# A two-layer conditioned token mixer on one core: fourteen groups of unread matmuls left out, and the last tiles' steps placed anew

## The chip, the cores and the metric

The kernel runs on one core of one Trainium2 chip. The metric is the device time of one execution in microseconds (us). Before the change three timed runs gave 438.00, 437.63 and 439.25 us, so the median is 438.0 us.

## The reference, cut to what matters

Two layers act on x (2 batches of 1024 tokens, 256 features), with one condition vector and 154 context rows per batch.

```python
# layer 0: attention over the context, router, gate and three experts
nx = layer_norm(x) * gamma + beta
weights = softmax((nx @ Wq) @ (context @ Wk).T / 16)
evidence = weights @ (context @ Wv)
combined = concat([nx, evidence, condition])            # 768 features
probs = softmax(combined @ router_W + router_b)         # 3 experts
h = silu(combined @ e_w1[e] + e_b1[e])                  # 512 per expert
routed = sum_e probs[e] * (h @ e_w2[e] + e_b2[e])
g = sigmoid(silu(combined @ gate_w1 + gate_b1) @ gate_w2 + gate_b2)
x = x + g * (routed @ out_w + out_b)
# layer 1: adaptive layer norm, attention with 16 heads of 16 features
q = ada_ln(x, condition) @ Wq + bq
k, v = split(ada_ln(context, condition) @ Wkv + bkv)
x = x + concat_heads(softmax(q k.T / 4) v) @ Wp + bp
```

The output is x, in f32.

## The kernel before

The 2048 tokens are cut into 8 tiles of 256 (t from 0 to 7, four to a batch). Weights, keys and values are prepared once and stay in the on-chip memory. Many products are made exact by splitting both operands into a high and a low part and taking three products, high by high, low by high and high by low (the helper `exact`, lines 1688, 1689 and 1690).

For each tile the work runs through these steps, named in the code by a short key. A key such as ("score", 6, 3) means step score of tile 6, part 3.

- Layer 0: ln, norm, low, att, prob, route and logit make the normalized tokens, their attention over the context and the router. za and z fill one of two hidden banks on TensorE in two halves, in seven units u. ScalarE (also called z) takes the tanh, VectorE (z) finishes the silu, ScalarE (h) makes the high part, GpSimd (h) the low part, and TensorE multiplies both (p) into the token bank. evac adds the token bank to the expert sum. init puts the router-weighted expert biases into that sum, on VectorE, lines 1395 and 1397. res closes the layer.
- Layer 1: qn, shift, xhat, qx, qlow and query normalize the tokens anew and make the queries. stack copies them with DMAs into the stacked form. most computes scores of head pairs and VectorE takes the maximum of each. row turns these maxima around. score computes the scores again with the maxima subtracted, twelve parts of a 128x512 bank, and ScalarE takes their exponential into a ring of six. value multiplies by the values, four parts. raw copies out, sum adds up the softmax denominators (GpSimd), sums is their reciprocal, dup and out spread and multiply them (VectorE), out on ScalarE makes the high part, outl on VectorE the low part, and proj is the last product. For the last tile proj is cut into lead (its first two groups of heads) and last (the other two, in two halves of tokens). Each ends with an addition to the tokens on VectorE and a DMA to the output.

Layer 0 of tile t runs beside layer 1 of tile t-1. After the last part of ("p", 7, 6) nothing of layer 0 is left, and TensorE has only layer 1 of tiles 6 and 7.

**What sets the order.** Nothing is scheduled at run time. Each step has a slot, a number: FIRST + 14 t plus the number in PLAN, or in PLAN_OF for a single tile. For each engine the slot plus the number in DELAY is sorted, and the steps are written in that order into the engine's own instruction stream. Only the relative size of the numbers matters. Each step waits on semaphores for what it reads and for the buffers that it overwrites. Three banks of scores are shared by most, row and score in that order of use, so a score waits until the step three places before it has been read.

**fill.** The step fill, on TensorE alone, is a group of four products of 128x128 by 128x256 into the token bank (line 2129). Nobody reads them, and no semaphore is signalled. There are 14 groups with slots 120.23 to 131.47, all behind ("evac", 7, 3), the last reader of the token bank. Groups 0 to 6 stand among the scores of tile 6, groups 7 and 8 among those of tile 7, and groups 9 to 13 ahead of ("proj", 6).

## Time and profile before

| | |
|---|---|
| median of three runs | 438.0 us (437.63 to 439.25) |
| the profiled execution's own time | 439.08 us |
| its span, first to last instruction | 436.9 us |
| TensorE matmul busy | 422.1 us, 97% |
| TensorE weight load busy | 384.7 us, 88% |
| VectorE busy | 296.3 us, 68% |
| ScalarE busy | 223.6 us, 51% |
| GpSimd busy | 175.0 us, 40% |
| mean granted TensorE clock | 0.996 of full |

In the profile PE is TensorE's matmul, PEld its weight load, DVE is VectorE, ACT is ScalarE, POOL is GpSimd and SP is the engine that issues DMAs. The clock is a share of full speed: 1.00 is 2.4 GHz and 0.50 is 1.2 GHz. Busy time says what an engine did, not what set the end. A matmul's row spans its whole latency, so rows that follow each other overlap, and the pace is the distance of their starts.

### The profile page before, as it was taken

The numbers are of one execution on the slowest core, as the hardware profiler recorded it, in microseconds if no ns is written. First come the engines' busy times: TensorE is split into PE (matmuls) and PEld (weight loads), VectorE is DVE, ScalarE is ACT, GpSimd is POOL, SyncE is SP. The second block draws the span as 40 slices with busy tenths as digits, with TensorE's granted clock in tenths as the row PEclk, the third lists the DMA queues.
The fourth block names the chain that finished last, engine by engine and source line by source line (L and its number), as shares of the span: only waits on it lengthen the run. The fifth ranks groups of instructions, "written<-read, shape, count | busy, mean of one in ns | idle before, by whom it ended". The sixth has DMA issues, their size and how long they took to land.

```text
span 436.9 us, 9623 instructions
## 1 busy us (share of the span) xinstructions
PE 422.1 (97%) x3629; PEld 384.7 (88%) x3629; DVE 296.3 (68%) x748; ACT 223.6 (51%) x487; POOL 175.0 (40%) x184
## 2 busy tenths in 40 slices
PE   7899999999999999999999999999999899979996
PEld 6578999989998899889998899889988898868876
DVE  2785566674675696739863797389658755891797
ACT  2868643255347543764367246724672356326271
POOL 4545474553353526324523344344433632330020
PEclk9999999999999999999999999999999999998999
DMA  8786102531100210023000300030003021300301
GB/s 288 252 298 269 50 2 47 142 91 31 44 5 1 63 59 30 24 78 116 2 5 13 109 1 5 14 86 0 5 20 80 0 56 28 80 3 26 72 3 48
DMA packets 16837, 27.80 MB, mean 64 GB/s; under 512 B 3800, under 2 KB 9112, under 8 KB 16664
## 3 DMA queue, kind: packets, MB, share of 16 engines
q1 hardware_dynamic: 16664, 27.19, 21.2%
q8 instruction: 29, 0.48, 0.5%
q14 instruction: 16, 0.13, 0.1%
q10 hardware_dynamic: 128, 0.01, 0.0%
HBM read 15.94 MB, written 2.10 MB: 41 GB/s over the span
## 4 chain that ended last, share of the span: by engine, by line
PE 77%; DVE 15%; issue 3%; ACT 3%; DMA 1%; SPq 1%; ACTq 0%
PE hidden_banks L1688 7%; PE hidden_banks L1690 7%; PE hidden_banks L1689 7%; PE score_banks L1695 6%; PE score_banks L2060 5%; PE token_bank L1688 5%; PE token_bank L1689 5%; PE token_bank L1690 5%; PE score_banks L2030 4%; PE value_bank L2083 3%; PE value_bank L2086 3%; PE value_bank L1695 3%; DVE head_maxima L1463 3%; PE hidden_banks L1913 2%; DVE sums L1477 2%
## 5 line engine op out<-in xcount | busy, mean ns | idle before, releaser
L1620 POOL TENSOR_TENSOR hidden_low<-hidden,hidden_high 128x512 fp32r<-128x512 f32 x56 | 72.8, 1300 | 123.5 <-ACT hidden_high L1072 123.4
L1463 DVE TENSOR_REDUCE head_maxima<-score_banks 128x2 f32<-128x308 f32 x128 | 54.6, 473 | 17.1 <-PE score_banks L2030 15.0
L1688 PE MATMUL hidden_banks<-normed_high,hidden_w_high 128*128 128x256 f32 x224 | 64.2, 287 | 0.8 <-issue 0.8
L1689 PE MATMUL hidden_banks<-normed_high,hidden_w_low 128*128 128x256 f32 x224 | 62.5, 279 | 0.0
L1690 PE MATMUL hidden_banks<-normed_low,hidden_w_high 128*128 128x256 f32 x224 | 62.5, 279 | 0.0
L1132 ACT ACTIVATE exp_ring<-score_banks 128x512 f32<-128x512 f32 x96 | 52.6, 600 | 18.8 <-PE score_banks L2060 17.5
L1072 ACT CAST hidden_high<-hidden 128x512 fp32r<-128x512 f32 x56 | 34.8, 622 | 48.2 <-DVE hidden L1380 48.1
L1688 PE MATMUL token_bank<-expert_out_high,hidden_high 128*128 128x256 f32 x192 | 55.7, 290 | 0.0
L1064 ACT ACTIVATE hidden<-hidden_banks 128x512 f32<-128x512 f32 x56 | 33.3, 595 | 41.6 <-PE hidden_banks L1913 40.0
L1690 PE MATMUL token_bank<-expert_out_low,hidden_high 128*128 128x256 f32 x192 | 53.4, 278 | 0.0
L1689 PE MATMUL token_bank<-expert_out_high,hidden_low 128*128 128x256 f32 x192 | 53.4, 278 | 0.0
L1380 DVE SCALAR_TENSOR_TENSOR hidden<-hidden,hidden_banks 128x512 f32<-128x512 f32 x56 | 38.2, 683 | 18.5 <-ACT hidden L1064 18.3
L1688 PEld LDWEIGHTS hidden_banks<-normed_high,hidden_w_high 128*128 128x128 f32 x224 | 42.1, 188 | 2.1 <-issue 2.0
L1689 PEld LDWEIGHTS hidden_banks<-normed_high,hidden_w_low 128*128 128x128 f32 x224 | 42.3, 189 | 0.1
L1690 PEld LDWEIGHTS hidden_banks<-normed_low,hidden_w_high 128*128 128x128 f32 x224 | 42.0, 188 | 0.0
L1688 PEld LDWEIGHTS token_bank<-expert_out_high,hidden_high 128*128 128x128 f32 x192 | 36.2, 188 | 0.5 <-issue 0.2
L1689 PEld LDWEIGHTS token_bank<-expert_out_high,hidden_low 128*128 128x128 f32 x192 | 36.3, 189 | 0.2
L1690 PEld LDWEIGHTS token_bank<-expert_out_low,hidden_high 128*128 128x128 f32 x192 | 36.1, 188 | 0.0
L2030 PE MATMUL score_banks<-pair_keys,query_stack 96*128 96x308 f32 x112 | 29.4, 335 | 2.5 <-DVE head_maxima L1463 1.4
L1913 PE MATMUL hidden_banks<-probs_T_tail,context_w_tail 100*128 100x256 f32 x112 | 31.6, 282 | 0.0
L1689 PE MATMUL hidden_banks<-probs_T_high,context_w_low 128*128 128x256 f32 x112 | 31.2, 279 | 0.0
L1688 PE MATMUL hidden_banks<-probs_T_high,context_w_high 128*128 128x256 f32 x112 | 31.2, 279 | 0.0
(294 smaller groups left out, 1111.5 us busy)
## 6 DMA issues: line engine op xcount, KB each, us to landing
unit_weights<-units SPq DMA_DIRECT2D x7, 768.0 KB, 6.0
query_stack<-queries_high SPq DMA_DIRECT2D x56, 64.0 KB, 2.0
tokens<-x SPq DMA_DIRECT2D x8, 256.0 KB, 3.7
query_stack<-queries_low SPq DMA_DIRECT2D x28, 64.0 KB, 2.0
w_slice<-units SPq DMA_DIRECT2D x7, 256.0 KB, 3.0
out<-tokens SPq DMA_DIRECT2D x7, 256.0 KB, 2.4
w_T<-folds SPq DMA_DIRECT2D x6, 256.0 KB, 6.1
pair_keys<-keys_high SPq DMA_DIRECT2D x16, 77.0 KB
```

What stands on the lines that cost most here:

```text
L1064: nc.scalar.activation(TB[:, ring(t, u), :], Z[:, hidden_bank(t, u), :], ACT.Tanh, scale=0.5).then_inc(scalar_z, 1)
L1072: nc.scalar.copy(SH[:, ring(t, u), :], TB[:, ring(t, u), :]).then_inc(scalar_h, 1)
L1132: nc.scalar.activation(E[:, w % ERING, :], S[:, ring_of[key][0], :], ACT.Exp).then_inc(scalar_score, 1)
L1380: v.scalar_tensor_tensor(out=TB[:, ring(t, u), :], in0=TB[:, ring(t, u), :], scalar=1.0, in1=Z[:, hidden_bank(t, u), :], op0=ALU.add, op1= ...
L1463: v.tensor_reduce(MX[:, s, first:first + step + 1:step], S[:, ring_of[key][0], 0:2 * CTX].rearrange("p (j n) -> p j n", j=2), AX.X, ALU.ma ...
L1620: nc.gpsimd.tensor_tensor(SL[:, ring(t, u), :], TB[:, ring(t, u), :], raw(SH[:, ring(t, u), :]), ALU.subtract).then_inc(gpsimd_h, 1)
L1688: mm(out_, lh, rh, start=start, stop=False, skip_group_check=skip)
L1689: mm(out_, ll, rh, start=False, stop=False, skip_group_check=skip)
L1690: return mm(out_, lh, rl, start=False, stop=stop, skip_group_check=skip)
L1695: last = mm(out_, l, r, start=(i == 0), stop=(i == len(pairs) - 1))
L1913: return mm(half, VWD[0:BROWS, b, c], PTD[0:BROWS, t % 2, :], start=False, stop=True)
L2030: mm(bank, QS[0:STACK, c, P * s:P * s + P], KS[b][0:STACK, c, :, :].rearrange("p j n -> p (j n)"), start=True, stop=True).then_inc(tensor_ ...
```

## The change

The step fill goes, with its constant, its placing loop and its function, and the tables that hold the slots get new numbers. The list of slots of fill stays in the table and is not read. The arithmetic of everything that is read stays as it is.

```diff
-FILLS = 14
@@
-        "h": 0.6, "ln": 0.86, "qn": -0.2, "low": 0.9, "keyn": 1.2, "split": 2.1,
+        "h": 0.6, "ln": 0.9, "qn": -0.2, "low": 0.9, "keyn": 1.2, "split": 2.1,
@@
-        "outl": (33.4, 33.8), "row": (19.96, 21.53), "h": 1.2, "p": 3.5, "last": (39.5, 39.7), "query": 18.06,
+        "h": 1.2, "out": (27.73, 34.37), "last": (45.1, 45.4), "sums": (29.6, 36.2), "qlow": 18, "ln": 0.6,
...
@@
-    for i in range(FILLS):
-        place(SETUP["fill"][i], ("fill", i))
-
@@
-            def fill(key):
-
-                if key[1] == 0:
-                    pe.wait_ge(vector_evac, upto(vector_evac, ("evac", LAST, EXPERTS), "o"))
-                for _ in range(4):
-                    mm(O[:, 0:TILE], WPh[:, 0, 0:P], WPh[:, 0, :], start=True, stop=True)
-
-            parts = {"warm": warm_up, "fill": fill, "cv": context_v, "ck": context_k, ...
+            parts = {"warm": warm_up, "cv": context_v, "ck": context_k, ...
```

**TensorE, tile 6's scores.** The rows begin with the scores (line 2060) that follow proj of tile 5. Line 2129 is fill, 1980 is ("qx", 7), 2083 and 2086 are value. Before:

```order
L2060 MATMUL score_banks<-query_stack,pair_keys_67 128x256 x6
L2129 MATMUL token_bank<-proj_w_high 128x256 x8
L2060 MATMUL score_banks<-query_stack,pair_keys_67 128x256 x6
L2129 MATMUL token_bank<-proj_w_high 128x256 x8
L1980 MATMUL head_bank<-constants,x_hat_171 128x128 x4
L2083 MATMUL value_bank<-exp_ring,head_values_69 32x256 x4
L2086 MATMUL value_bank<-exp_ring,head_values_tail_71 32x256 x4
```

Now (line numbers from here to the end are three lower than before):

```order
L2057 MATMUL score_banks<-query_stack,pair_keys_67 128x256 x12
L1977 MATMUL head_bank<-constants,x_hat_171 128x128 x4
L2080 MATMUL value_bank<-exp_ring,head_values_69 32x256 x4
L2083 MATMUL value_bank<-exp_ring,head_values_tail_71 32x256 x4
L2080 MATMUL value_bank<-exp_ring,head_values_69 32x256 x4
```

The sixteen unread products are gone, and the rest stands in the same order. After ("query", 7), the next twelve (line 2129 x4 and x8) go in the same way, and the six products of scores 9 to 11 stand directly ahead of the maxima of tile 7.

**VectorE, the end.** The rows begin with the second shuffle of tile 7 (line 1486). Line 1477 is the reciprocal, 1506 is outl, 1518 the addition of tile 6, 1512 those of tile 7. Before:

```order
L1486 STREAM_SHUFFLE last_outs_twice<-last_outs_and_sums 128x512
L1477 RECIPROCAL last_sums<-last_sums 128x256
L1496 STREAM_SHUFFLE last_sums_spread<-last_sums 128x256 x2
L1498 TENSOR_TENSOR last_outs_twice<-last_outs_twice,last_sums_spread 128x512
L1506 SCALAR_TENSOR_TENSOR last_outs_low<-last_outs_high,constants,last_outs_twice 128x512 x2
L1518 TENSOR_TENSOR tokens<-tokens,head_bank 128x512
L1512 TENSOR_TENSOR tokens<-tokens,hidden_banks 128x256 x2
```

Now:

```order
L1483 STREAM_SHUFFLE last_outs_twice<-last_outs_and_sums 128x512
L1503 SCALAR_TENSOR_TENSOR last_outs_low<-last_outs_high,constants,last_outs_twice 128x512
L1474 RECIPROCAL last_sums<-last_sums 128x256
L1493 STREAM_SHUFFLE last_sums_spread<-last_sums 128x256 x2
L1495 TENSOR_TENSOR last_outs_twice<-last_outs_twice,last_sums_spread 128x512
L1515 TENSOR_TENSOR tokens<-tokens,head_bank 128x512
L1503 SCALAR_TENSOR_TENSOR last_outs_low<-last_outs_high,constants,last_outs_twice 128x512
L1509 TENSOR_TENSOR tokens<-tokens,hidden_banks 128x256 x2
```

The first of the two outl of tile 7 moved ahead of the last reciprocal, and tile 6's addition moved ahead of the second.

**VectorE, init of tile 7.** The rows begin with the shift of tile 6 (line 1439). Line 1380 is z, here ("z", 7, 2), 1395 and 1397 are init, 1447 is qlow. Before:

```order
L1439 SCALAR_TENSOR_TENSOR shift_85<-mean_var_83,rstd_84 128x2
L1380 SCALAR_TENSOR_TENSOR hidden<-hidden,hidden_banks 128x512
L1395 TENSOR_SCALAR expert_sum<-expert_bias,router_probs 128x256 x2
L1397 SCALAR_TENSOR_TENSOR expert_sum<-expert_bias,router_probs,expert_sum 128x256 x2
L1397 SCALAR_TENSOR_TENSOR expert_sum<-expert_bias_177,router_probs,expert_sum 128x256 x2
L1447 SCALAR_TENSOR_TENSOR query_in_low<-head_bank,modulation,query_in_high 128x256 x2
```

Now:

```order
L1436 SCALAR_TENSOR_TENSOR shift_85<-mean_var_83,rstd_84 128x2
L1392 TENSOR_SCALAR expert_sum<-expert_bias,router_probs 128x256 x2
L1394 SCALAR_TENSOR_TENSOR expert_sum<-expert_bias,router_probs,expert_sum 128x256 x2
L1394 SCALAR_TENSOR_TENSOR expert_sum<-expert_bias_177,router_probs,expert_sum 128x256 x2
L1377 SCALAR_TENSOR_TENSOR hidden<-hidden,hidden_banks 128x512
L1444 SCALAR_TENSOR_TENSOR query_in_low<-head_bank,modulation,query_in_high 128x256 x2
```

init moved ahead of z. On TensorE ("qx", 6) moved ahead of ("value", 5, 0), and on ScalarE ahead of the exponential of ("score", 5, 5). A few more neighbours of tiles 5 and 6 change places: za of tile 6 (u 3 and 4) with a score of tile 4, h of tile 6 (u 1 to 3) with a neighbour on ScalarE, prob of tile 7 with maxima of tile 5 and z, att and ln of tile 6 by one or two places. GpSimd and SP keep their orders.

## Rows read from the trace of the kernel before

**Rows 1.** The page: busy time by engine; the chain's shares by engine.

```profile
PE 422.1 (97%) x3629; PEld 384.7 (88%) x3629; DVE 296.3 (68%) x748; ACT 223.6 (51%) x487; POOL 175.0 (40%) x184
...
PE 77%; DVE 15%; issue 3%; ACT 3%; DMA 1%; SPq 1%; ACTq 0%
```

**Rows 2.** Timeline of PE: start, us, line, tiles, count, idle before.

```profile
393.68 0.98 PE L2060 MATMUL score_banks<-query_stack,pair_keys 100*128 100x256 f32 x6 [1.67 <-DMA query_stack<-max_low]
394.49 1.78 PE L2129 MATMUL token_bank<-proj_w_high 128*128 128x256 f32 x8
...
398.62 0.60 PE L1980 MATMUL head_bank<-constants,x_hat 128*128 128x128 f32 x4
...
401.01 0.98 PE L2060 MATMUL score_banks<-query_stack,pair_keys 100*128 100x256 f32 x6
```

**Rows 3.** Stretches of PE: from:to, length, busy (count), clock, DMA share, GB/s.

```profile
391.85:393.68 1.83, 0.16 (x3) 1.00 0.04 9
393.68:394.66 0.98, 0.98 (x8) 0.99 0.00 0
394.66:398.05 3.39, 3.39 (x18) 0.50 0.24 80
...
398.05:405.54 7.49, 7.49 (x80) 1.00 0.01 2
405.54:414.97 9.43, 9.43 (x85) 1.00 0.37 83
```

**Rows 4.** Timeline of ACT in the same stretch.

```profile
394.28 1.57 ACT L1132 ACTIVATE exp_ring<-score_banks 128x512 f32<-128x512 f32 x3 [5.33 <-PE score_banks L2060]
395.73 1.10 ACT L1089 ACTIVATE x_hat<-tokens,shift,rstd 128x256 f32<-128x256 f32 x2
396.80 1.58 ACT L1132 ACTIVATE exp_ring<-score_banks 128x512 f32<-128x512 f32 x3
399.25 0.84 ACT L1098 ACTIVATE query_in_high<-head_bank,modulation 128x256 fp32r<-128x256 f32 x2 [0.88 <-PE head_bank L1980]
```

**Rows 5.** Timeline of DVE in the same stretch.

```profile
404.31 0.88 DVE L1455 SCALAR_TENSOR_TENSOR queries_low<-head_bank,query_bias,queries_high 128x256 fp32r<-128x256 f32 x2 [3.31 <-ACT queries_high L1110]
```

**Rows 6.** The chain that ended last, near the end: start, us, what.

```profile
415.45 0.38 ACT max_halves L1121
...
431.19 0.67 DVE last_outs_low L1506
...
431.90 0.39 PE hidden_banks L2094
...
434.18 0.13 PE hidden_banks L2095
```

**Rows 7.** Timeline of PE near the end.

```profile
426.20 2.66 PE L2129 MATMUL token_bank<-proj_w_high 128*128 128x256 f32 x20
428.70 0.28 PE L2094 MATMUL head_bank<-proj_w_high,next_outs_low 128*128 128x256 f32 x1
```

**Rows 8.** Timeline of DVE near the end.

```profile
432.54 0.68 DVE L1518 TENSOR_TENSOR tokens<-tokens,head_bank 128x512 f32<-128x512 f32 x1
```

**Rows 9.** Timeline of DVE at init, tile 6 first, then tile 7.

```profile
320.41 1.80 DVE L1397 SCALAR_TENSOR_TENSOR expert_sum<-expert_bias,router_probs,expert_sum 128x256 f32<-128x256 f32 x4
...
359.75 0.69 DVE L1380 SCALAR_TENSOR_TENSOR hidden<-hidden,hidden_banks 128x512 f32<-128x512 f32 x1 [0.74 <-ACT hidden L1064]
360.36 0.61 DVE L1395 TENSOR_SCALAR expert_sum<-expert_bias,router_probs 128x256 f32<-128x256 f32 x2
361.00 2.82 DVE L1397 SCALAR_TENSOR_TENSOR expert_sum<-expert_bias,router_probs,expert_sum 128x256 f32<-128x256 f32 x4
```

**Rows 10.** Timeline of POOL at init of tile 7.

```profile
361.27 1.35 POOL L1620 TENSOR_TENSOR hidden_low<-hidden,hidden_high 128x512 fp32r<-128x512 f32 x1 [2.46 <-ACT hidden_high L1072]
```

**Rows 11.** Timeline of ACT at init of tile 7.

```profile
360.58 0.61 ACT L1072 CAST hidden_high<-hidden 128x512 fp32r<-128x512 f32 x1
...
363.19 0.84 ACT L1098 ACTIVATE query_in_high<-head_bank,modulation 128x256 fp32r<-128x256 f32 x2 [0.68 <-PE head_bank L1980]
```

More of the change, by code:

```diff
@@ L292 @@
     0: {
-        "most": (21.92, 23.13, 24.17, 24.59, 25.33, 27.11, 27.44, 28.14), "qlow": 19.3, "query": 19.9, "qn": 17.5,
-        "h": 1.3, "qx": 18.7, "xhat": 18.2,
+        "h": 1.3, "query": 19.9, "qx": 18.7, "qn": 17.5, "xhat": 18.2,
+        "most": (21.92, 23.13, 24.17, 24.59, 25.33, 27.11, 27.44, 28.14), "qlow": 19.3,
     },
@@ L305 @@
     6: {
-        "init": 6.5, "score": (30.5, 30.6, 30.6, 31.3, 31.4, 31.6, 31.9, 31.9, 31.9, 32.5, 32.6, 33),
-        "raw": (34.4, 34.5), "proj": 47.7, "most": (21.9, 22, 24.8, 25.8, 26.5, 27.3, 27.4, 28), "ln": 0.9,
-        "value": (31.83, 31.84, 34.15, 34.75), "norm": 1.79, "stack": (16.3, 16.7, 21.5, 21.9),
-    },
-    7: {
-        "route": 13.2, "most": (19.2, 19.2, 19.3, 19.4, 19.4, 19.6, 20.3, 20.5), "init": 5.6, "sums": (28.4, 36),
-        "za": -0.73, "score": (22.06, 22.59, 22.73, 23.07, 23.16, 23.16, 23.63, 23.73, 24.03, 24.23, 24.34, 24.54),
-        "outl": (33.4, 33.8), "row": (19.96, 21.53), "h": 1.2, "p": 3.5, "last": (39.5, 39.7), "query": 18.06,
-        "xhat": 17.7, "ln": 0.5, "value": (23.2, 23.5, 24.7, 25.8), "proj": 38, "logit": 14.9, "out": (27.3, 33.2),
-        "raw": (23.1, 28.7), "qlow": 18, "qx": 17.62, "dup": (24.9, 28.7), "step": 1.96,
+        "value": (31.83, 31.84, 34.15, 34.75), "att": 7.5, "stack": (16.4, 16.7, 21.5, 21.9), "init": 6.6,
+        "raw": (34.2, 34.5), "h": 1.4, "proj": 48.9, "za": -0.6,
+        "score": (30.5, 30.6, 30.6, 30.9, 31.1, 31.3, 31.9, 31.9, 31.9, 32.5, 32.6, 33),
+        "most": (21.9, 22, 24.8, 25.8, 26.5, 27.3, 27.4, 28), "qx": 19.4,
+    },
+    7: {
+        "h": 1.2, "out": (27.73, 34.37), "last": (45.1, 45.4), "sums": (29.6, 36.2), "qlow": 18, "ln": 0.6,
+        "value": (23.31, 23.4, 25.91, 26.08), "raw": (23.5, 29.1),
+        "score": (22.2, 22.7, 22.9, 23.1, 23.2, 23.3, 23.8, 23.8, 24.2, 24.4, 24.5, 24.7), "dup": (25.7, 29.7),
+        "step": 1.96, "za": -0.73, "outl": (32.2, 36.4), "route": 13.2, "p": 3.5, "prob": 9.9, "row": (19.99, 21.56),
+        "xhat": 17.6, "most": (19.2, 19.2, 19.3, 19.4, 19.5, 19.5, 20.3, 20.5), "query": 18, "qx": 17.6,
     },
@@ L319 @@
     "vw": (1.6, 3, 3.8, 4.5, 6.1, 7.7, 8.2), "vt": (0.8, 2, 2.9, 3.9, 7.1, 9.1, 10.7),
-    "unit": (0.99, 2.23, 3.75, 4.08, 9.23, 9.4, 9.94), "w2": (7.4, 10.3, 11.1, 13, 14.2, 17.9), "norm": -0.3,
-    "low": 1.7, "att": 2, "prob": 2.8, "route": 3.8, "logit": 4.75, "cb": 4.3, "bq": 12.2, "split": (8.74, 13.12),
+    "unit": (1, 2.2, 3.8, 4.1, 9.2, 9.4, 9.9), "w2": (7.4, 10.3, 11.1, 13, 14.2, 17.9), "norm": -0.3, "low": 1.7,
+    "att": 2, "prob": 2.8, "route": 3.8, "logit": 4.75, "cb": 4.3, "bq": 12.2, "split": (8.74, 13.12),
     "keyn": (11.4, 12.5), "keyx": (12.4, 13.8), "key": (13.4, 17.8), "mod": (9.2, 9.6, 10.3, 10.6), "ck": 10.8,
-    "fold": (0.6, 12), "late": (6.6, 14.9), "ln": -6.8, "silu": -0, "group": 1.1, "gsplit": 5.6, "setup2": -12,
+    "fold": (0.6, 12), "late": (6.6, 14.9), "ln": -6.8, "silu": 0, "group": 1.1, "gsplit": 5.6, "setup2": -12,
     "bias1": -7.9,
-    "fill": (120.23, 120.27, 120.77, 120.82, 121.09, 121.76, 121.98, 127.05, 127.63, 128.86, 129.54, 129.71, 131.45, 131.47),
+    "fill": (120.2, 120.3, 120.8, 120.8, 121.1, 121.8, 122, 127, 127.6, 128.9, 129.5, 129.7, 131.4, 131.5),
     "sel": 114.7, "unstack": 105, "bias2": (26.4, 26.7), "zero": 102.7,
@@ L2122, in last_proj @@
                 proj_part(LAST, s, range(GROUPS // 2, GROUPS)).then_inc(tensor_last, 1)
[L2124 to L2131 removed]
+            parts = {"warm": warm_up, "cv": context_v, "ck": context_k, "fold": fold, "vw": context_w, "vt": context_tail, "w2": w2, "cb": bias_out, "mod": mod, "bq": query_bias,
                      "keyx": keyx, "key": pair_keys, "bias2": expert_bias, "norm": norm, "att": att, "prob": prob, "logit": logit,
```

1 line of the change is left out of this document (removed).

## The prediction

> **What bounds the kernel now.** I read the page first: TensorE is busy 422.1 of 436.9 us and holds 77% of the chain that ended last, VectorE 15% [rows 1]. A product taken away is therefore worth something only where TensorE is itself what the next step waits for, and the 56 unread products stand in the last 45 us, where layer 0 has ended and the work is thin. So I then read the timelines of the engines there, the stretches with the granted clock, and last the chain. Two places matter.
>
> First, tile 6's scores, 393.68 to 405.54. TensorE stood idle from 391.85 to 393.68 waiting for the maxima's DMA, did six scores in 0.98, and then issued eight unread products, six scores, eight unread products, and the transposes of qx [rows 2]. The clock was 0.99 in the first 0.98 us, 0.50 (1.2 GHz) from 394.66 to 398.05, and 1.00 (2.4 GHz) afterwards [rows 3]. ScalarE had no pause between 394.28 and 398.38: three exponentials, x_hat, three exponentials [rows 4].
>
> Second, from about 416 to 431.86 the chain runs on VectorE almost without a break, started by ScalarE's max_halves at 415.45, and TensorE takes over at 431.90 for the last 18 products [rows 6].
>
> **The change part by part.** The sum is made against the profiled execution, 439.08 us.
>
> 1. *Fill groups 0 to 6, tile 6.* Their 28 products stand on TensorE in four places; the first eight took 1.78 us, mostly at half clock [rows 2, 3], and at full clock four take 4 x 0.12, about 0.5 us (the pace in [rows 6]). What comes off the path is less, since other engines set the pace there. ScalarE is full until 396.80 + 1.58 = 398.38 whatever TensorE does, so the next step, query_in_high, can move from 399.25 to 398.4 and no further: 0.9 [rows 4]. Its transposes can start when x_hat is done (395.73 + 1.10 = 396.83) and take 0.60 at full clock [rows 2]; at half clock 1.2, so 398.03, still in time. Behind them come two value parts (together the 1.8 us from the transposes' end, 398.62 + 0.60, to the six scores at 401.01; 1.0 each when apart) and six scores of 0.98 [rows 2]. If the clock is back at 398.05 as before, they end at 398.05 + 2.0 + 0.9 = 400.95, and query starts then instead of at 401.01 + 0.98 = 401.99: 1.05. All that hangs on query moves by this: queries_low ended at 404.31 + 0.88 = 405.19 [rows 5] and now ends at 404.15. Before, the maxima of tile 7 began at 405.54, where a stretch of rows 3 begins, because the last three fill groups and scores 9 to 11 stood ahead of them. Now only queries_low holds them: 404.15. Gain 1.4. The bounds: had the clock never dropped, value would start at 397.4, its second part would wait for the exponentials until 398.4, the scores would end at 400.3, and the maxima begin at 403.5, a gain of 2.0. With the clock low until about 401.5, the transposes and value would end only at about 401.8, scores 402.7, query 404.1, maxima 406.0, which is 0.45 later than before. I take 1.4, the case of rows 3 as they are.
>
> 2. *The maxima of tile 7*, 405.54 to 414.97, 9.43 us at clock 1.00 with no gap [rows 3]. Nothing is removed here, the stack DMAs are issued by the same step and move with it. Cost 0.
>
> 3. *Fill groups 7 to 13.* Worth 0 on the path: the five last groups took 2.66 us and pushed proj of tile 6 to 428.70 [rows 7], but the end waits for VectorE's out and outl until 431.86 [rows 6]. The cover is VectorE's chain; without it the 2.5 us from 426.20 to 428.70 would be the most to gain, and VectorE does not let it through.
>
> 4. *VectorE's new order at the end.* The first outl of tile 7 (0.67 in the chain) now delays the last reciprocal and what follows by 0.6 to 0.67. It had stood in the shadow of ScalarE's cast, which is now covered by tile 6's addition (0.68) instead [rows 6, 8]. Then the second outl ends at about 431.86 + 0.6 + 0.65 = 433.1 instead of 432.5. TensorE has lead behind it already and only 8 of 18 products left. At the chain's 0.12 apiece [rows 6] they end at 434.35, where the 18 ended at 434.31. Cost 0.05; bounds -0.6 (if the swap costs nothing and ten products go) and +0.6.
>
> 5. *TensorE's clock at the end.* No row shows TensorE without the fill there. Before, 20 unread products filled 426.20 to 428.70 [rows 7]. Now it will stand idle there until tile 6's outl is done, do proj and lead, and stand idle again some 2 us before the last eight products. An idle time of 1.83 us was followed by half clock one microsecond after work had begun again [rows 3]. If the last eight products run at half clock they cost 8 x 0.12 = 0.95 more; if not, 0. I take the middle, 0.45.
>
> 6. *init ahead of ("z", 7, 2).* init can start where VectorE was idle ahead of z, at 359.75 - 0.74 = 359.0, and lasts 0.61 + 1.80 (as in tile 6) [rows 9]. z (0.69) then ends at about 362.2 instead of 360.44. Behind it on ScalarE wait the cast of 0.61, an exponential of 0.5 [rows 4] and query_in_high: 362.2 + 0.6 + 0.5 = 363.3 instead of 363.19 [rows 11]. Cost 0.1. The 2.82 of tile 7 stood beside 1.35 of GpSimd's hidden_low [rows 10], and that now waits for the cast, behind init. Were it 2.82 all the same, the cost is 1.1, the upper bound. TensorE has the other half of z to do meanwhile and idles for 0.2 at most in my case. The other swaps of tiles 5 and 6 exchange neighbours of 0.4 to 0.8 us; I price them at 0, within 0.5 either way (about one exponential, 1.57 / 3 [rows 4]).
>
> The Trainium skill, SBUF — State Buffer, section "Who interferes with whom", says that a VectorE instruction with both inputs in SBUF contends with a GpSimd instruction that reads SBUF. The trace agrees (2.82 beside GpSimd against 1.80 without). By that rule init is the short one, the 0.1 above; if the 1.02 had another cause, it would be the 1.1.
>
> Sum: 439.08 - 1.4 + 0 + 0.05 + 0.45 + 0.1 = 438.3. The profiled execution is 1.08 above the median of the three runs, which gives 437.2 when the same -0.8 is taken from 438.0. Runs that never saw the half clock have less fill time to give back than this one, and may be those near 437.6. I forecast between the two: 437.7.
>
> **The rivals.**
>
> *A: the full clock stays or is kept early.* Part 1 gives 2.0, part 5 nothing: 439.08 - 2.0 + 0.15 = 437.2, on the median 436.1. For it: the unread products were themselves slowed and lengthened that stretch. Against it: the idle 1.83 us ahead of the scores remains, and less work follows it.
>
> *B, slower: the low clock lasts.* In the stretch 394.66 to 398.05 TensorE was busy 3.39 of 3.39 us and the full clock came back at its end [rows 3]. Without fill it has only scores and transposes there, with gaps for ScalarE, some 2.5 us of work. If the clock then stays at 1.2 GHz until about 401.5, part 1 costs 0.45: 439.08 + 0.45 + 0.05 + 0.45 + 0.1 = 440.1, on the median 439.0. If a low stretch of 3.4 us falls into the maxima of tile 7 too, these lose half of it, 1.7: 441.8 and 440.7. It decides at whether the value parts of tile 6 run at half clock; from there on the change loses.
> The Trainium skill, TensorE: Matmul & The Clock Gate, Part 1, says that the throttled state is the default and activity releases it. That speaks for B, and the trace agrees as far as it goes: 0.50, then 1.00 after a stretch of full work.
>
> *C: the new order in tiles 5 to 7 decides.* init's upper bound or a swap that TensorE waits for: up to 1.1 + 0.5 on top of the forecast, 439.3 on the forecast's scale; or 0.5 less, 437.2. TensorE's high busy share speaks for little slack to gain.
>
> **How the numbers follow.** Forecast 0.45, A 0.17, B 0.28 (0.13 of it with the second low stretch), C 0.10. A change under 0.5%, 2.2 us, cannot be told from none. Faster than 435.8 needs A with the lower bounds of parts 4 and 6: 0.10. Slower than 440.2 is the worse half of B and a little of C: 0.15. The rest, 0.75, is no change. The range runs from A less 0.4, 435.7, to the worse case of B on the median's scale, 440.7. The forecast's own range is 437.2 to 438.3.
>
> **What would show it.** After the change, TensorE's scores, transposes and value of tile 6 without line 2129; query_in_high 4.1 us after the first exponential instead of 5.0; the maxima of tile 7 beginning about 10.5 us after the first score instead of 11.9; and 9.4 us for the maxima. Clock 0.50 between the first scores and the value parts and 1.00 behind would bear out part 1; 1.00 all along is A, 0.50 in the value parts is B. In the end VectorE still dense for 16 us, idle TensorE ahead of proj and of the last eight products, these at 0.12 apiece or 0.24. init with 1.80, and query_in_high of tile 6 not over 0.2 later than before. The prediction is wrong if the maxima of tile 7 begin as late as before, or if the end no longer waits for VectorE.

## The result, and the profile after

The kernel after takes 440.92 us (median of 20 executions, 439.61 to 443.32), the kernel before 438.70 us (median of 20). The ratio is 1.0050, 95% interval 1.0032 to 1.0068: 2.2 us slower. I had forecast 437.7 us and no change. The profiled execution after took 442.21 us, its span is 440.1 us, 3.15 us more than the one read before (436.94), and its mean granted clock is 0.981.

The page of the kernel after: busy time, the chain's shares, and the granted clock in 40 equal slices. In the kernel after, the lines of the engines' code lie three lower than in [rows 1 to 11].

```profile
PE 421.9 (96%) x3573; PEld 381.7 (87%) x3573; DVE 294.9 (67%) x748; ACT 223.1 (51%) x487; POOL 176.0 (40%) x184
PE 72%; DVE 17%; ACT 4%; issue 4%; DMA 2%; SPq 1%; POOL 0%; ACTq 0%; POOLq 0%
PEclk9899989999999999999999999999999999996998
```

56 products are gone, and TensorE is busy only 0.2 us less [rows 1]: the busy time of the products that were left out came back as products that ran longer at half clock. TensorE's share of the chain fell by 5 points, VectorE's, ScalarE's and the DMAs' rose. The clock line has four low places: two early ones, one in tile 6, one near the end.

Tile 6, timeline of TensorE after. It answers to [rows 2].

```profile
396.50 3.03 PE L2057 MATMUL score_banks<-query_stack,pair_keys 100*128 100x256 f32 x12 [1.66 <-DMA query_stack<-max_low]
399.71 1.12 PE L1977 MATMUL head_bank<-constants,x_hat 128*128 128x128 f32 x4 [0.17 <-ACT x_hat L1086]
400.75 1.08 PE L2080 MATMUL value_bank<-exp_ring,head_values 128*32 128x256 f32 x8
...
404.18 0.97 PE L2057 MATMUL score_banks<-query_stack,pair_keys 100*128 100x256 f32 x6
...
408.45 0.38 PE L1685 MATMUL score_banks<-last_keys_high,queries_high 128*128 128x308 f32 x1 [1.19 <-ACT exp_ring L1129]
```

The same place in stretches (from:to, length, busy time and count by engine, clock, DMA share, GB/s). It answers to [rows 3].

```profile
394.84:396.50 1.66, 0.00 (x1) 0.00 (x0) 1.53 (x6) 0.00 (x0) 0.00 (x0) 1.00 0.05 10
396.50:397.12 0.62, 0.62 (x5) 0.62 (x6) 0.00 (x0) 0.01 (x1) 0.57 (x1) 1.00 0.00 0
397.12:403.95 6.83, 6.56 (x46) 3.81 (x44) 1.63 (x4) 4.73 (x10) 0.13 (x1) 0.50 0.13 42
403.95:408.45 4.50, 3.31 (x31) 2.92 (x25) 0.88 (x2) 3.42 (x8) 0.00 (x0) 1.00 0.00 0
408.45:417.83 9.38, 9.38 (x82) 7.78 (x82) 7.32 (x17) 1.31 (x3) 0.74 (x1) 1.00 0.37 84
```

The half clock came 0.6 us into the scores (1.0 before) and lasted 6.83 us in place of 3.39 [rows 3]. The transposes took 1.12 instead of 0.60 [rows 2] and each full group of eight value products 1.08. The maxima of tile 7 began 408.45 - 396.50 = 11.95 us after the first score. My forecast was 10.5. They lasted 9.38, as forecast.

ScalarE and VectorE in tile 6, answering to [rows 4, 5]:

```profile
397.11 1.57 ACT L1129 ACTIVATE exp_ring<-score_banks 128x512 f32<-128x512 f32 x3 [5.32 <-PE score_banks L2057]
400.97 0.88 ACT L1095 ACTIVATE query_in_high<-head_bank,modulation 128x256 fp32r<-128x256 f32 x2
404.78 1.57 ACT L1129 ACTIVATE exp_ring<-score_banks 128x512 f32<-128x512 f32 x3 [2.93 <-PE score_banks L2057]
```
```profile
407.48 0.88 DVE L1452 SCALAR_TENSOR_TENSOR queries_low<-head_bank,query_bias,queries_high 128x256 fp32r<-128x256 f32 x2 [4.72 <-ACT queries_high L1107]
```

query_in_high starts 3.9 us after the first exponential (4.1 forecast), so the step ahead of the value parts came out as I had worked it out. Then ScalarE waits 2.93 us for scores that stand behind 3.4 us of value products at half clock (400.75 to 404.18).

Tile 5, TensorE after, and init on VectorE (answering to [rows 9]):

```profile
283.75 1.31 PE L1692 MATMUL head_bank<-score_w,normed 128*128 128x157 f32 x8
...
286.07 0.40 PE L2057 MATMUL score_banks<-query_stack,pair_keys 100*128 100x256 f32 x2
...
288.14 0.55 PE L2027 MATMUL score_banks<-pair_keys,query_stack 96*128 96x308 f32 x2 [0.67 <-DMA query_stack<-queries_high]
```
```profile
362.57 1.80 DVE L1394 SCALAR_TENSOR_TENSOR expert_sum<-expert_bias,router_probs,expert_sum 128x256 f32<-128x256 f32 x4
```

The first row is the step att of tile 6, which now stands ahead of ("za", 5, 4) and of ("score", 3, 11); the last one of TensorE is the first pair of maxima of tile 4, which now waits for a stack DMA. init took the 1.80 that I forecast.

The end: the first and the last pieces on VectorE and TensorE of the chain that ended last (answering to [rows 6]), one row of TensorE's timeline (to [rows 7]), and one stretch.

```profile
418.45 0.38 ACT max_halves L1118
...
435.43 0.76 DVE last_outs_low L1503
...
436.24 0.39 PE hidden_banks L2091
...
437.33 0.13 PE hidden_banks L2092
```
```profile
430.28 0.39 PE L2091 MATMUL head_bank<-proj_w_high,next_outs_low 128*128 128x256 f32 x1 [1.83 <-DVE next_outs_low L1503]
```
```profile
431.20:434.80 3.60, 3.60 (x20) 3.60 (x19) 3.52 (x8) 0.02 (x1) 0.00 (x0) 0.53 0.02 5
```

TensorE idled 1.83 us ahead of proj, ran at half clock from 431.25 to 434.66, and was back at full clock for the last eight products (0.12 apiece). VectorE was busy 3.52 of these 3.60 us: the low clock there lies beside VectorE's chain.

**Where the 3.15 us are.** One step marks each tile on VectorE: its queries_low. I cut both executions there (before, after, difference):

| stretch | before | after | difference |
|---|---|---|---|
| start to tile 0's | 103.65 | 105.37 | +1.72 |
| tile 0's to tile 3's | 132.69 | 132.71 | +0.02 |
| tile 3's to tile 4's | 44.39 | 44.64 | +0.25 |
| tile 4's to tile 5's (att moved) | 43.23 | 44.27 | +1.04 |
| tile 5's to tile 6's (init moved) | 43.62 | 43.42 | -0.20 |
| tile 6's to tile 7's (scores of tile 6) | 36.73 | 37.07 | +0.34 |
| tile 7's to the end | 32.63 | 32.61 | -0.02 |

The 1.72 stands where no instruction was moved; two low stretches of the clock lie in it. I took it for a matter of that execution. Whether it is, and what an execution of the kernel before usually looks like in tile 6, needed more executions.

### The profile page after: what moved, and what is told of

It is laid out like the page before. It is cut to its first block, busy times and chain, and to the rows that moved or that the text cites. A ratio compares the mean times of both kernels' runs of the same rounds, so it can differ in the third digit from the quotient of the medians.

```text
span 440.1 us, 9511 instructions
## 1 busy us (share of the span) xinstructions
PE 421.9 (96%) x3573; PEld 381.7 (87%) x3573; DVE 294.9 (67%) x748; ACT 223.1 (51%) x487; POOL 176.0 (40%) x184
## 4 chain that ended last, share of the span: by engine, by line
PE 72%; DVE 17%; ACT 4%; issue 4%; DMA 2%; SPq 1%; POOL 0%; ACTq 0%; POOLq 0%
PE hidden_banks L1685 7%; PE hidden_banks L1687 6%; PE hidden_banks L1686 6%; PE score_banks L1692 6%; PE token_bank L1685 4%; PE score_banks L2057 4%; PE token_bank L1686 4%; PE token_bank L1687 4%; PE score_banks L2027 3%; DVE head_maxima L1460 3%; PE value_bank L2080 3%; PE value_bank L1692 3%; PE value_bank L2083 3%; PE hidden_banks L1910 2%; DVE sums L1474 2%
```

## The experiments

My theory after the traces: the change costs in two places, att's early place (1.0 us) and the clock of tile 6. The rival was that only one of them is real. A third reading, my forecast's, was that the products only cost time. The first four kernels split the change.

**e1: no unread products, old order.**

```diff
-FILLS = 14
+FILLS = 0
```

> The kernel before with all 56 unread products left out and nothing else changed. Theory: half of the loss is the TensorE clock, which without the unread products stays at half through tile 6's scores and value parts, so that the maxima of tile 7 still begin 11.9 us after the first score and the last eight products run slower; the order is the old one, so nothing is lost around 283 us. Expected ratio to before 1.000 to 1.002 (0 to +0.8 us). Rival: the whole loss is the missing products (clock); then the ratio is 1.005 (+2.2 us) here. Second rival, the one I had forecast: the products only cost time, and leaving them out gives 1.4 us, ratio 0.997.

Measured: ratio 1.0047 (1.0029 to 1.0065), 440.45 us. More than my own theory gave (1.000 to 1.002), near the rival's 1.005. Leaving out the products costs about 1.8 us of mean span by itself (2.2 in the medians), and my forecast's reading has fallen.

**e2: new order, products kept.**

```diff
-    "fill": (120.23, 120.27, 120.77, ..., 127.05, 127.63, 128.86, ...),
+    "fill": (119.8, 119.82, 120.77, ..., 127.25, 127.75, 129.1, ...),
 PLAN_OF = {   # tiles 0, 6 and 7 as in the kernel after
```

> The new order of tiles 5 to 7 on every engine, but with the 56 unread products kept at their old neighbours on TensorE. Theory: the moved steps are the larger half, most of it the step att of tile 6 that now stands ahead of two others at 283 us and costs 1.1 us there; expected ratio to before 1.0025 to 1.004 (+1.1 to +1.7 us). If the missing products are the whole loss, the ratio is 1.000. The stretch from the first score of tile 6 to the maxima of tile 7 should last 11.9 us with clock 1.00 after about 3.4 us of half clock.

Measured: 1.0058 (1.0036 to 1.0081) from six executions. Its trace has 44.16 us in the stretch of att (43.23 before), and full clock in tile 6: first score to maxima 10.29 us, not the 11.9 with a half clock that I had expected. e1 and e2 add up to twice what the kernel after loses, and each is uncertain by 0.8 us or more. e2's mean clock is 0.992, and none of its six executions has the full clock; the sorting by clock below leaves it 0.9 us, within 0.5, at equal clock, as much as e4. Why its clock is low is open: its trace has 3.4 us of half clock in the setup and 2 us at the end.

**e3: the kernel after, att at its old place. e4: the kernel before, att at the new place.**

```diff
-        "value": (31.83, 31.84, 34.15, 34.75), "att": 7.5, "stack": ...
+        "value": (31.83, 31.84, 34.15, 34.75), "stack": ...
```

> The kernel after, with only the step att of tile 6 put back behind the twelfth score of tile 3 on TensorE (and behind the eviction evac 5 1 on VectorE). Theory: this swap is the 1.1 us that the traces show between 281 and 289 us; expected 1.1 us faster than the kernel after, ratio to before about 1.0025 (+1.1 us), and the value parts and maxima at 284 to 290 without the idle of 0.5 us and more ahead of them. Rival: the 1.1 us was already lost elsewhere (a late DMA or a clock dip of that execution); then the ratio stays at 1.005.

Measured: 1.0062 (1.0039 to 1.0085). The time did not show the 1.1 us; the trace did: 43.19 us in the stretch of att (44.27 after). Tile 6 had 6.8 us of half clock, 12.44 us from first score to maxima.

> The kernel before, with only the step att of tile 6 moved ahead of za 5 4 and the twelfth score of tile 3 on TensorE (and ahead of evac 5 1 on VectorE), as in the kernel after. Theory: +1.1 us, ratio 1.0025, all of it lost between 281 and 289 us. Rival: the swap alone is harmless, ratio 1.000.

Measured: 1.0032 (1.0014 to 1.0050), 44.15 us in the stretch. The sum that I expected held here. How the loss comes about, in the kernel before with att early: SyncE's queue, one piece of the chain, TensorE's timeline.

```profile
282.93 0.59 SPq L870 DMA_DIRECT2D query_stack<-queries_low  x1
283.56 2.25 SPq L870 DMA_DIRECT2D query_stack<-queries_high  x2
```
```profile
283.56 3.07 DMA query_stack<-queries_high
```
```profile
286.68 0.55 PE L2030 MATMUL score_banks<-pair_keys,query_stack 96*128 96x308 f32 x2 [0.55 <-DMA query_stack<-queries_high]
```

And its transfers from 283.5 to 286.7 (queue, packets, MB, share; then issues: count, KB each, median us from issue to landing):

```profile
q8 instruction: 1, 0.02, 2.6%
...
query_stack<-queries_high SPq DMA_DIRECT2D x3, 64.0 KB, 3.0
```

The kernel before at this place: SyncE's queue, the transfers from 282.88 to 285.05, TensorE's timeline, and the transfers from 279 to 281.

```profile
282.88 1.22 SPq L870 DMA_DIRECT2D query_stack<-queries_high  x2
```
```profile
query_stack<-queries_high SPq DMA_DIRECT2D x3, 64.0 KB, 2.0
```
```profile
282.88 1.24 PE L1695 MATMUL head_bank<-score_w,normed 128*128 128x157 f32 x8
...
285.05 0.55 PE L2030 MATMUL score_banks<-pair_keys,query_stack 96*128 96x308 f32 x2
```
```profile
q8 instruction: 1, 0.02, 3.8%
```

The DMA that the maxima need took 3.07 us instead of 2.0, and one packet of instructions (16 KB) lies among the stack copies; in the kernel before it came at about 279.7, ahead of them. The traces divide the same way. In all five with att early (the kernel after twice, e2, e4, e10) the packet stands 1.0 to 1.7 us behind the first copy's issue, and SyncE took 1.88 to 2.33 us for the two issues of the row above. In all fifteen with att late it stands 1.9 us or more ahead of the first copy, and the two issues took 1.22. Among the five, the wait of the maxima follows the packet's own time: 0.67 us where the packet took 1.55, 0.15 where it took 1.1. Of the 0.9 us that the stretch grew in e4, 0.55 is the wait; the rest is TensorE's own, which reaches the maxima 4.71 us after queries_low's start instead of 4.32. That att's place costs this time is shown by e3 and e4. That the packet delays the copy is what the coincidence suggests; no run isolates it.

**What the executions say together.** Every execution has a span and a mean granted clock, so they can be sorted. The 134 executions of the kernel before that ran beside my kernels:

| mean clock | executions | mean span |
|---|---|---|
| 1.000 | 54 | 435.8 |
| 0.995 to 0.996 | 56 | 436.8 |
| 0.992 | 20 | 437.2 |
| 0.988 | 4 | 439.4 |

One low stretch of 3.4 us takes 0.5 x 3.4 / 437 = 0.004 off the mean clock. A least-squares fit through all executions of all kernels, with one slope and an offset for each kernel, puts the price of one at 0.8 us on average; the steps of the table are uneven (1.0, 0.4, 2.2). The kernel before holds the full clock in four of ten executions. The kernel after never did: its 31 executions have a mean clock of 0.987 and a mean span of 438.7, against 436.5 for before. e1 stands at 0.9875, e4 at 0.995. By that fit e1 at full clock would equal the kernel before (-0.3 us, within 0.5): all its loss goes with the clock. e4's does not (+1.0, within 0.4). The kernel after would stand at +0.1, within 0.3. So nearly all of its loss goes with the clock too, and att's cost does not show in its times; it is read from the traces, where gains of 0.2 us (init) and 0.35 us (the products, below) stand against it.

Both traces of the kernel after that I read are among its lowest clocks: 0.981 and 0.979, as in 6 of its 31 executions; the other 25 lie at 0.986 to 0.995. The 6.8 us of tile 6 and 3.4 us near the end alone would give about 0.988, so most of its executions can have had no low stretch in the setup.

**e5 and e6: one half of the products each.** e5 leaves out the 28 of tile 6, e6 the 28 near the end.

```diff
-    "fill": (120.23, 120.27, ..., 121.98, 127.05, 127.63, ..., 131.47),
+    "fill": (127.05, 127.63, ..., 131.47),      # e5, FILLS = 7
+    "fill": (120.23, 120.27, ..., 121.98),      # e6, FILLS = 7
```

> The kernel before with only the 28 unread products of tile 6 left out (those near the end stay). The runs so far: leaving out all 56 costs 1.8 us of span, and the mean granted clock falls from 0.997 to 0.987, while runs of one clock take the same span. Theory: the products of tile 6 prevent the half clock there; without them the profile shows 0.50 for 6.8 us (or 3.4 us in every execution) from about 397 us, mean clock about 0.993, span +0.8 to +1.2 us, ratio 1.002 to 1.003. Rival: the products near the end matter, and this one is at 1.000 with the clock of before, 0.997.

Measured: 1.0039 (1.0024 to 1.0053), mean clock 0.991, span +1.6, more than the 0.8 to 1.2 expected. Its trace: 11.40 us from the first score to the maxima.

> The kernel before with only the 28 unread products near the end left out (those of tile 6 stay). Theory: a low stretch of 3.4 us near the last products appears in every execution and costs about 0.8 us; mean clock about 0.992, ratio 1.002. Rival: VectorE holds the end and the clock there costs nothing: span as before, ratio 1.000, though the clock is lower.

Measured: 1.0019 (1.0005 to 1.0032), mean clock 0.992. Its trace shows 32.6 us from tile 7's queries_low to the end, as before, and full clock in tile 6; its low stretches are 6.8 us in the setup and the last 1.4 us. In no trace of any run does the low clock near the end cost more than 0.2 us, yet the median of e6 is 0.7 us up. One trace does not settle that; it stays open.

**e7 and e8: products in the wait.** TensorE idles 1.7 us for the maxima's DMA ahead of the scores. e7 adds 12 unread products there; e8 has these 12 in place of tile 6's 28.

```diff
+    "fill": (119.0, 119.05, 119.1, 120.23, ..., 131.47),   # e7, FILLS = 17
+    "fill": (119.0, 119.05, 119.1, 127.05, ..., 131.47),   # e8, FILLS = 10
```

> The kernel before with 12 more unread products (1.4 us) in the wait of 1.7 us ahead of tile 6's scores. Theory: the low clock of tile 6 comes from that idle time; with it filled, the clock stays at 1.00 there in all executions, mean clock 0.998 or more, span 0.3 to 0.6 us shorter than before, ratio 0.999. Rival: the sparse work behind it causes the low clock, and nothing changes (0.997, ratio 1.000); or the products delay the scores, ratio 1.001.

Measured: 0.9999 (0.9988 to 1.0011), mean clock 0.997; 7 of 12 executions at 1.000. As the rival had it: no change in the time.

> As the kernel without tile 6's unread products (those near the end stay), but with 12 unread products in the wait ahead of tile 6's scores. If the idle time ahead of the scores brings the half clock, it is gone here, mean clock 0.997 or better, and the gain that I had forecast for leaving the products out between the scores shows: 1 us less than before, ratio 0.998. If the sparse scores, transposes and value parts bring it, it is as in the kernel with none of tile 6's products: clock 0.993, ratio 1.002 to 1.003.

Measured: 0.9987 (0.9968 to 1.0007), mean span 435.8, 8 of 12 executions at clock 1.000. TensorE's timeline in e8, then its stretch, then the same stretch in a second trace of the kernel before (e15) and in the first one:

```profile
392.38 1.60 PE L2129 MATMUL token_bank<-proj_w_high 128*128 128x256 f32 x12
394.23 0.99 PE L2060 MATMUL score_banks<-query_stack,pair_keys 100*128 100x256 f32 x6 [0.24 <-DMA query_stack<-max_low]
395.48 1.48 PE L2060 MATMUL score_banks<-query_stack,pair_keys 100*128 100x256 f32 x6 [0.27 <-ACT exp_ring L1132]
397.43 0.66 PE L1980 MATMUL head_bank<-constants,x_hat 128*128 128x128 f32 x4 [0.47 <-ACT x_hat L1089]
...
404.17 0.38 PE L1688 MATMUL score_banks<-last_keys_high,queries_high 128*128 128x308 f32 x1 [1.19 <-ACT exp_ring L1132]
```
```profile
394.23:404.17 9.94, 8.02 (x73) 5.84 (x73) 2.51 (x6) 8.16 (x18) 0.70 (x1) 1.00 0.09 29
```
```profile
393.38:403.67 10.29, 10.29 (x101) 9.16 (x101) 2.51 (x6) 8.17 (x17) 0.70 (x1) 1.00 0.08 28
```
```profile
393.68:405.38 11.70, 11.70 (x100) 10.61 (x101) 2.51 (x6) 8.37 (x17) 0.70 (x1) 0.85 0.08 25
```

This is the main reading. The wait is filled up to its last 0.24 us, the work behind it is the same as in the kernel after, with gaps (8.02 of 9.94 us busy), and the clock stays at 1.00. With the clock equal, 28 products cost 10.29 - 9.94 = 0.35 us and not 1.4 (e7, with the wait filled too, has 10.29). And the trace that I forecast from was one with the half clock: another execution of the same kernel needs 1.41 us less.

The time from the first score of tile 6 to the first product of the maxima of tile 7, in all traces:

| clock in the stretch | with tile 6's 28 products | without |
|---|---|---|
| 1.00 throughout | 10.29 (e2, e6, e7, e15) | 9.94 to 9.95 (e8 to e12, e17, e18) |
| half for 3.4 us | 11.70, 11.71 (before, e4) | 11.11 to 11.55 (e1, e16, e5, e13) |
| half for 6.8 us | none | 11.95 to 12.44 (after, e14, e3) |

With the wait filled, eight of nine traces have the full clock in tile 6 (not e13's). With the wait open and no products behind it, none of six has; with the wait open and the 28 products behind it, three of five have. The half clock did not begin with the work: in these traces it came 0.6 to 2.9 us after the first score (0.6, 1.3 and 1.8 in the new order, 2.3, 2.4 and 2.9 in e1, e16 and e5), and 3.3 us after it in e13. So filling the wait keeps the clock up in most executions; how the wait and the work behind it share in the fall is not shown.

The Trainium skill, TensorE: Matmul & The Clock Gate, section "HAM oscillation — how this bites in real kernels", tells of a wait for data between groups of matmuls after which the next group starts throttled. The runs here agree that the wait matters, and differ in that the clock was 1.00 in the first 0.6 us and more of the next group.

**e9 and e17: the wait in the setup.** The same idea for the wait of 0.98 us at 8.1 us.

```diff
+                if b == 0:
+                    for _ in range(7):      # e17: range(2)
+                        mm(O[:, 0:TILE], SCW[0][:, 0, 0:P], SCW[0][:, 0, :], start=True, stop=True)
                 pe.wait_ge(scalar_ck, upto(scalar_ck, ("ck", b), "kT"))
```

> The kernel with 12 unread products in the wait ahead of tile 6's scores, none between them and the old 28 near the end (span 435.8 in the mean, at full clock in 8 of 12 executions, two low stretches in the other 4), and besides 7 unread products (0.8 us) in the wait of 0.98 us at 8.1 us of the setup. Theory: the low clock of the setup comes from that wait; filled, (nearly) all executions run at clock 1.000, mean span 435.4, ratio to before 0.998. Rival: the low clock there comes from the many small products and DMA waits behind it; still a third of the executions at 0.992, mean span 435.8 or more, ratio 0.9987.

Measured: 1.0023 (1.0003 to 1.0044). My product was mis-sized. TensorE's timeline in e9:

```profile
9.01 3.18 PE L1727 MATMUL token_bank<-context_and_value_w 128*128 128x256 f32 x14
```

Seven products are 14 instructions and last 3.18 us, and tile 0's queries_low came at 107.35 us instead of 104.23 (e8). Filling the wait with two of them instead:

> As the kernel with 7 unread products in the wait of the setup, with 2 of them: the 7 took 3.18 us in place of the 0.8 that I had reckoned (each is two instructions of 0.23), so that 2 take 0.9 and fit the wait of 0.98. Theory: the low stretches of the setup and at 60 us come from that wait and go: clock 1.000 in nearly all executions, mean span 435.4, ratio 0.998. Rival: no link; a third of the executions at 0.992 as without them, 435.8, ratio 0.9987; each 0.1 us of products that outlast the wait is added.

Measured: 0.9980 (0.9963 to 0.9997), mean clock 0.9987; 8 of 12 executions at 1.000, the other four at 0.996. Without the two products (e8) four had been at 0.992. It looks as if one of two low stretches went, not both, but the time is not told apart from e8's (0.9987).

**e10: the kernel after with the filled wait.** e11: also att back and the 28 products near the end. e12: the old order, the filled wait, and only the 20 last products. e13: as e11, with only these 20.

```diff
+    "fill": (119.0, 119.05, 119.1),                                   # e10
+    "fill": (119.0, 119.05, 119.1, 127.25, 127.75, 129.1, ...),       # e11, "att": 7.5 removed
+    "fill": (119.0, 119.05, 119.1, 128.86, 129.54, ..., 131.47),      # e12
+    "fill": (119.0, 119.05, 119.1, 129.1, 129.54, ..., 131.47),       # e13, "att": 7.5 removed
```

> The kernel after, with 12 unread products in the wait ahead of tile 6's scores and nowhere else. Theory: the two low stretches of tile 6 go, clock from 0.987 to about 0.994, the maxima of tile 7 begin 10.5 us after the first score as I had forecast for the kernel after, and the span falls by 1.5 to 2 us: mean span 437.0, ratio to before 1.001 to 1.002. Rival: the half clock comes all the same a little later, since the work is as sparse as in the kernel after: 438.7, ratio 1.005.

Measured: 1.0004 (0.9986 to 1.0022), mean span 436.7. Twelve products in one wait give back 2 us of the 2.2 that the change cost. att still costs: 43.75 us in its stretch, with 0.15 us of waiting for the copy.

> The new order of tiles 5 to 7 but with att of tile 6 at its old place, 12 unread products in the wait ahead of tile 6's scores and the 28 near the end. Against the kernel with the old order and the same unread products (mean span 435.8, ratio 0.9987) this shows what the rest of the new order is worth: 0 to +0.3 us by the runs so far, ratio 0.9987 to 0.9995. If the end's new order brings a low stretch of its own, clock 0.994 and ratio 1.001.

Measured: 0.9979 (0.9961 to 0.9997), 437.92 us. The rest of the new order costs nothing: 43.36 us where init moved against 43.63 in e8, and 32.57 against 32.41 at the end.

> The old order, 12 unread products in the wait ahead of tile 6's scores, and of the 28 near the end only the 20 that stand after the last value part; the 8 between the scores of tile 7 go. Theory: these 8 only delay the value parts by about 1 us behind VectorE's chain and fill no wait: span unchanged to -0.3 us, clock as with all 28, ratio 0.998 to 0.9987. Rival: without them a low stretch comes near the end: clock lower by 0.004, ratio 1.000.

Measured: 0.9986 (0.9964 to 1.0007). As expected.

> The new order of tiles 5 to 7 with att of tile 6 at its old place, 12 unread products in the wait ahead of tile 6's scores, and 20 behind the last value part; none between scores. Theory: the pieces add up: mean span 435.5 to 435.8, ratio to before 0.998, and 0.993 to 0.995 to the kernel after. Rival: the 8 products left out between tile 7's scores matter in the new order: clock 0.996 or lower where 1.000 is the most frequent, ratio 1.000.

Measured: 0.9994 (0.9977 to 1.0011), and no execution over 0.997. Its trace has the half clock of tile 6 in spite of the filled wait (11.55 us) and 4.7 us of it at the end. e13 differs from e11 only in 8 products that stand behind tile 6's scores, so this cannot be laid on its edit. The pieces did not add up; the filled wait makes the low clock rare, not impossible.

**e14, e15, e16: second traces** of the kernel after, the kernel before and e1.

> The kernel after once more, beside the others on one chip. Ratio 1.005 as before. In its trace: half clock for 6.8 us in tile 6's scores (stretch from the end of tile 6's queries_low to tile 7's about 37.1 to 37.6 us), tile 5's queries_low to tile 6's 44.2 us. The low stretches of the setup and of 59 us, which another trace of it shows, need not be there; if they are, they belong to the change after all and not to the execution.

Measured: 1.0047 (1.0031 to 1.0062). Its trace: half clock for 6.8 us in tile 6 again (12.23 us), 43.85 us in the stretch of att, 105.36 us to tile 0's queries_low, with 6.8 us of low clock in the setup.

> The kernel before once more, for a second trace. By the clocks of its many runs it holds the full clock in about 4 of 10 executions and in tile 6 in most of them: then the stretch from tile 6's queries_low to tile 7's is 35.35 us in place of the 36.73 of the trace read before. If it is 36.7 again, the half clock of tile 6 is its usual course.

Measured: 437.37 us. Full clock in tile 6 (the row of 10.29 us above), and 3.4 us of half clock in the setup. So low stretches of the setup come in executions of the kernel before too. And e16 below is the same kernel as e1: tile 0's queries_low starts at 103.97 us in one trace and at 105.63 in the other, which has 6.8 us of low clock ahead of it. The 1.72 us are thus the execution's, not the change's. The low clock is not their only source: e18's trace has the full clock there and 105.68, with 1.2 us of TensorE waiting for VectorE's expert_out_low.

> The kernel before without all its unread products, a second trace. The first had 3.4 us of half clock in tile 6 and 36.3 us from tile 6's queries_low to tile 7's; the kernel after has 6.8 us and 37.1 to 37.6. If the length is a matter of the execution, this trace can show either; the full clock all along (35.1) would speak against the theory.

Measured: 438.10 us. Stretches of e16: before, in and behind the half clock.

```profile
393.37:395.70 2.33, 2.05 (x11) 1.46 (x11) 0.76 (x2) 1.72 (x4) 0.70 (x1) 1.00 0.01 4
395.70:399.20 3.50, 3.21 (x22) 1.81 (x26) 0.45 (x2) 3.02 (x7) 0.00 (x0) 0.51 0.25 80
399.20:404.50 5.30, 4.12 (x45) 3.29 (x37) 1.30 (x4) 3.43 (x8) 0.00 (x0) 1.00 0.00 0
```

3.4 us again. In three traces of the old order without tile 6's products it lasts 3.4 us, in three of the new order 6.8 us (e13, new order with the filled wait, has 3.4). Six traces are too few to lay this on the order.

**e18: the pieces that held, together.** e11 and the two products of e17.

> The new order of tiles 5 to 7 with att of tile 6 at its old place, 2 unread products in the wait of the setup, 12 in the wait ahead of tile 6's scores, 28 near the end. Theory: the stretch from tile 5's queries_low to tile 6's is 43.2 us, the next 43.4, the next 35.1, the clock 1.000 in most executions; mean span 435.4 to 435.6, ratio to before 0.997 to 0.998. Rival: the wait's products and the order do not add, 0.9987 or more.

Measured: 0.9983 (0.9960 to 1.0006), 437.96 us; 7 of 12 executions at clock 1.000, three more at 0.998. The stretches are 43.15, 43.41 and 35.07 us, as expected. By its ratio it is about 0.7% below the kernel after, and no better than e11 or e17. These two, and they only, are faster than the kernel before by more than their uncertainty, by 0.2%, and barely: both intervals end at 0.9997.

## Why the prediction was wrong

**Part 1, tile 6, -1.4 forecast: the step that failed.** "If the clock is back at 398.05 as before" did not hold. Before, the clock was back 4.4 us after the first score; in the kernel after it came back 7.5 and 8.1 us after it, and in the other traces without the products and with the wait open (e1, e16, e5, e3) 5.8 to 8.6 us after it. So the value parts ran at half clock, which is where I had put the decision of rival B. The maxima began 11.95 and 12.23 us after the first score in the kernel after; B's bound said 12.3. The term is +0.3 against the trace that I read, in place of -1.4. The end that I kept for the range was right, and I gave it 0.28. I had taken the return of the clock as given, though the products that I removed were part of the work ahead of it.

A smaller error stands in the same part: 405.54 is where a stretch of rows 3 begins, but the first product of the maxima starts at 405.38, 11.70 us after the first score and not 11.9. My own working gives -1.2 from there.

**The ground of the sum.** As large an error: I subtracted from one execution with the half clock in tile 6. Four of ten executions of the kernel before never leave the full clock, and a second trace passes the place in 10.29 us instead of 11.70. Against that course the kernel after loses 1.7 to 1.9 us in tile 6. The prediction had the remark that runs which never saw the half clock have less to give back, and used it for nothing but the middle of the forecast. What it should have asked is what holds the clock up in those runs.

**The size of the products.** At equal clock the 28 products cost 0.35 us, not 1.05 to 1.4: ScalarE's exponentials set the pace of the stretch, as [rows 4] showed. Rival A's -2.0 holds against the half-clock trace (11.70 - 9.94 = 1.76) and is -0.35 against the full-clock one.

**Part 2**, the maxima at 9.4 us: right (9.38, 9.34).

**Parts 3 to 5, the end, +0.5 forecast, 0 to 0.15 measured.** VectorE's chain covers it. The half clock came, at another place than feared (proj and the first part of lead, not the last eight products). The chain from max_halves to the last product is 437.46 - 418.45 = 19.0 us, against 18.9 before [rows 6].

**Part 6, the new order.** init was right in its 1.80 and wrong in its sign by a little: the stretch is 0.2 us shorter, not 0.1 longer. GpSimd's hidden_low now starts at 365.70, behind init. The rule of the Trainium skill, SBUF — State Buffer, section "Who interferes with whom", by which it was the short one, is borne out. "I price them at 0, within 0.5 either way", said of the other swaps, failed: att costs 0.5 to 1.0 us, and it lasts 1.24 us, not the 0.4 to 0.8 that I gave the swapped steps. I looked at the lengths of the exchanged steps and not at the DMA that lands beside them. The first maxima of tile 4 started about 0.2 us after their copy landed (282.88 + 2.0, then 285.05), so there was no slack for it.

**The sum.** 0.5 to 1.0 (att) - 0.2 (init) + 1.7 to 1.9 (tile 6 against its full-clock course) + 0 (the end) gives about 2.0 to 2.7, and less where the execution of the kernel before has the half clock in tile 6 too (0.3 for that term); measured 2.2 in the mean spans and in the medians. C and B were both true, and I had priced them as alternatives.

## What to carry to other kernels

Before you price a product that nobody reads as cost, ask what the clock does without it, and look at the granted clock of many executions, not of one trace: here the mean clock of each execution sorted the times, at about 0.8 us for each low stretch. If TensorE must idle for a DMA and the work behind has gaps, try filling that wait and not the work behind it; 12 products in the wait kept the clock up at least as often as 28 behind it (8 traces of 9, and 3 of 5), at 0.35 us less. When an order changes, compare the landing of each DMA with the start of what reads it: a copy that had landed about 0.2 us ahead of its reader kept it waiting up to 0.7 us once one step of TensorE had changed places.

## What the runs showed of the hardware

- Transfers of 16 KB of instructions (29 in one execution) changed their place when the order of the program changed. The one at tile 4's stack copies took 0.9 to 1.6 us. It stood among the copies in five of five traces with att early and ahead of them in fifteen of fifteen with att late. Where it fell among them, a copy landed after 3.1 us instead of 2.0 and the second of two issues took 1.6 us instead of 0.6 (e4).
- The half clock comes also in the setup, in traces of kernels with the same instructions there (before's second, e7), while TensorE is busy 3.27 to 3.50 of 3.50 us. In the first trace of the kernel after, in e1 and in e9 one low stretch began at 59 to 61 us, with no pause of TensorE in the 2 us ahead of it that the trace shows; nothing here explains it.
- A product of 128x128 by 128x256 whose operands are held in f32 as they come ran as two instructions of 0.23 us each at clock 1.00 (3.18 / 14, e9), where one of the fill, whose operand is held in the rounded type fp32r, is one instruction of 0.12.
- The price of a step beside another engine shows in init: 1.80 us for its four instructions with GpSimd's hidden_low behind them, 2.82 beside it.
